# Edge codes of the one-hot comparisons in f32, and the running sums of the last ten attribute batches on VectorE

## What is computed

```python
in_deg = jnp.minimum(jax.ops.segment_sum(ones, dst, num_segments=num_nodes), MAX_IN_DEGREE - 1)
out_deg = jnp.minimum(jax.ops.segment_sum(ones, src, num_segments=num_nodes), MAX_OUT_DEGREE - 1)
edge_proj = edge_attr @ W_sum + b_sum                             # 200000 edges, 128 attributes
sum3d = jax.ops.segment_sum(edge_proj, src, num_segments=num_nodes)
return x + z_in[in_deg] + z_out[out_deg] + cent_term + vor_term + sum3d
```

## Time and profile before

| | us |
|---|---|
| three timed runs | 5856.62, 5861.86, 5867.48 |
| median | 5861.86 |
| profiled execution | 5865.46 |
| its span, first to last instruction | 5863.7 |
| gathers of attribute rows, first to last issue | about 100 to 2163 |
| start of the node stage | about 2213 |

### The profile page before, as it was taken

The page is one execution under the profiler, slowest core; times in us unless marked ns, Lnnn a source line. Parts: engine busy times, 40 slices in busy tenths (PEclk is TensorE's granted clock), DMA queues, the critical chain, the costliest instruction groups (busy, mean ns, idle before and its releaser), DMA issues. The chain is left out here.

```text
span 5863.7 us, 46168 instructions
## 1 busy us (share of the span) xinstructions
PE 3804.6 (65%) x13508; PEld 2479.3 (42%) x13508; DVE 4214.6 (72%) x7748; ACT 1452.0 (25%) x4056; POOL 3577.6 (61%) x3626
## 2 busy tenths in 40 slices
PE   2777777986666655999997344444444444444899
PEld 1655666873444433666665111111111211112666
DVE  8575565559356606877774899999999999996334
ACT  1333333333333332322231111111111111111322
POOL 3777777777777765333321777777777777774000
PEclk9955555555555557999998677777777777776899
DMA  3444444444433332111211888888888888885000
GB/s 86 157 153 145 148 145 153 150 145 151 152 103 104 114 99 61 36 62 62 81 57 67 268 281 282 282 281 283 281 284 280 282 281 282 280 278 181 26 19 25
DMA packets 328215, 968.58 MB, mean 165 GB/s; under 512 B 84412, under 2 KB 124037, under 8 KB 315930
## 3 DMA queue, kind: packets, MB, share of 16 engines
q0 software_dynamic: 198672, 578.35, 32.3%
q1 hardware_dynamic: 80906, 211.35, 10.2%
q10 hardware_dynamic: 48384, 175.92, 7.7%
HBM read 670.63 MB, written 294.73 MB: 165 GB/s over the span
## 5 line engine op out<-in xcount | busy, mean ns | idle before, releaser
L598 POOL DMA_INDIRECT big<-in_edge_attr,big x1568 | 1579.1, 1007 | 573.3 <-issue 474.8
L1777 POOL DMA_INDIRECT big<-keys_values,idx x1674 | 1587.9, 949 | 509.9 <-issue 506.9
L2009 PE MATMUL bank<-big,ident 128*128 128x512 f32 x1674 | 953.1, 735 | 1155.7 <-DVE big L1859 1121.1
L905 PE MATMUL bank<-big,ident 128*128 128x128 f32 x3136 | 1188.0, 482 | 581.2 <-ACT bank L954 522.9
L905 PEld LDWEIGHTS bank<-big,ident 128*128 128x128 f32 x3136 | 777.0, 307 | 914.8 <-ACT bank L954 763.5
L2009 PEld LDWEIGHTS bank<-big,ident 128*128 128x128 f32 x1674 | 389.9, 240 | 1718.3 <-DVE big L1859 1227.3
L954 ACT ACTIVATE bank<-bank,big 128x128 f32<-128x128 f32 x1565 | 535.4, 342 | 1341.6 <-PE bank L905 1329.0
L1881 DVE TENSOR_TENSOR big<-big,bank 128x1536 f32<-128x1536 f32 x279 | 479.8, 1753 | 121.0 <-DMA big<-keys_values,idx 121.0
L651 DVE TENSOR_TENSOR big<-big 128x1024 bf16<-128x1024 bf16 x400 | 276.1, 690 | 342.1 <-PE bank L851 341.6
L1886 DVE TENSOR_REDUCE big<-big 128x48 f32<-128x1536 f32 x279 | 486.8, 1746 | 0.0
L1891 DVE TENSOR_TENSOR big<-big,bank 128x1536 f32<-128x1536 f32 x279 | 478.6, 1744 | 0.0
(11 more groups left out here) (360 smaller groups left out, 4473.2 us busy)
## 6 DMA issues: line engine op xcount, KB each, us to landing
running_sums<-big ACTq DMA_DIRECT2D x196, 512.0 KB, 2.8
running_attention<-big SPq DMA_DIRECT2D x46, 1632.0 KB, 7.6
queries_by_row<-big ACTq DMA_DIRECT2D x139, 512.0 KB
big<-queries_by_row SPq DMA_DIRECT2D x46, 1536.0 KB, 8.8
big<-keys_values,idx POOLq DMA_INDIRECT x1674, 3.9
big<-in_edge_attr,big POOLq DMA_INDIRECT x1568
keys_values<-big SPq DMA_DIRECT2D x7, 1792.0 KB, 7.1
x_after_layer<-big SPq DMA_DIRECT2D x7, 896.0 KB, 4.3
```

The costliest lines, as they stand in the source:

```text
L598: pool.indirect_dma_start(out=z.rows[:, r, k, :], out_offset=None, in_=w["edge_attr_128"][:, :], in_offset=bass.IndirectOffsetOnAxis(ap=z. ...
L905: pe.matmul(sum_of(k), lhsT=m.ident[:, :], rhs=z.rows[:, r, k, :], start=False, stop=True, skip_group_check=True).then_inc(s_sum, 1)
L1777: pool.indirect_dma_start(out=kv[:, r, k, :], out_offset=None, in_=t["kv"][:, :], in_offset=bass.IndirectOffsetOnAxis(ap=m.idx2[:, c:c + 1 ...
L2009: mm = pe.matmul(bank[pair % 4][:, :], lhsT=m.ident[:, :], rhs=kv[:, b % RINGK, i * S + j:(i + 1) * S + j + 1:S, D:KW], start=(j == 0), st ...
```

## The change

`z.nlo` and `z.nhi` are f32 in place of bf16. They take twice the bytes, and the ring of one-hot tables has 8 places in place of 10. The iota table and the one-hot tables remain bf16. Apart from that, the batches 186 to 195 (`DIRECT` = 10) are summed by VectorE: behind its side work one instruction for each column multiplies the sum of the column before by `goes1` and adds the gathered row, from PSUM and SBUF to PSUM. TensorE and ScalarE run their columns up to batch 185; ScalarE then has only the copies and stores of the last ten batches. A copy waits for one column more than it copies. The `due` list is made as before.

```diff
--- before.py
+++ after.py
@@ -54,11 +54,12 @@
 LM = max(PART_COLS)
 B1 = L1 // GB
 RING1 = 4
-RING_OH = 10
+RING_OH = 8
 HI = 50
 COUNTS_PER_TURN = (5, 11)
 READY = -1.0
 RATE = 8.2
+DIRECT = 10
 PLACES = P * L1
 SUMROWS = PLACES + P + 1
 
@@ -351,8 +352,8 @@
     z.zeros, at = cut(m.big, at, 1024)
     z.iota_jt, at = cut(m.big, at, P, GB, dt=BF16)
     z.zb, at = cut(m.big, at, P, dt=BF16)
-    z.nlo, at = cut(m.big, at, EC, dt=BF16)
-    z.nhi, at = cut(m.big, at, EC, dt=BF16)
+    z.nlo, at = cut(m.big, at, EC)
+    z.nhi, at = cut(m.big, at, EC)
 
     z.onehots = []
     for r in range(RING_OH - 2):
@@ -825,6 +826,16 @@
                     due.append(spent)
                 else:
                     spent += cost
+            for b in range(B1 - DIRECT, B1):
+                r = b % RING1
+                dve.wait_ge(s_g[r], 16 * GB * (b // RING1 + 1))
+                for k in range(GB):
+                    c = b * GB + k
+                    dve.wait_ge(s_sum, 2 + c)
+                    if k % GH == 0:
+                        dve.wait_ge(s_copied, 2 * (b - 1) + k // GH + 1)
+                    v.scalar_tensor_tensor(out=sum_of(k), in0=sum_of((k - 1) % GB), scalar=z.goes1[:, c:c + 1],
+                                           in1=z.rows[:, r, k, :], op0=ALU.mult, op1=ALU.add).then_inc(s_sum, 1)
             dve.wait_ge(s_found, 16 * NP1)
             for q in z.tails:
                 tail_places(dve, v, st, q, m.trash1[:, :])
@@ -896,7 +907,7 @@
                     yield
 
             work, placed = shadow(), 0
-            for b in range(B1):
+            for b in range(B1 - DIRECT):
                 r = b % RING1
                 pe.wait_ge(s_g[r], 16 * GB * (b // RING1 + 1))
                 for k in range(GB):
@@ -923,9 +934,9 @@
             qz = t["qrow"][0:ROWS, :].rearrange("(p k) d -> p (k d)", p=P)
             act.wait_ge(s_sum, 2)
 
-            def copy_half(b, k):
+            def copy_half(b, k, further=0):
                 r = b % RING1
-                act.wait_ge(s_sum, 2 + GB * b + GH * (k + 1))
+                act.wait_ge(s_sum, 2 + GB * b + GH * (k + 1) + further)
                 nc.scalar.activation(z.rows[:, r, GH * k:GH * (k + 1), :].rearrange("p k f -> p (k f)"), m.bank[2 + k][:, :],
                                      ACT.Copy).then_inc(s_copied, 1)
 
@@ -958,8 +969,12 @@
                         store(b - 1)
                     if k == GH:
                         copy_half(b, 0)
-            copy_half(B1 - 1, 1)
-            store(B1 - 1)
+            copy_half(B1 - DIRECT - 1, 1, 1)
+            store(B1 - DIRECT - 1)
+            for b in range(B1 - DIRECT, B1):
+                copy_half(b, 0, 1)
+                copy_half(b, 1, int(b < B1 - 1))
+                store(b)
             act.wait_ge(s_zero, 16 * ZEROS)
```

## The result

The changed kernel takes 5939.94 us in the median (5937.27 to 5942.43), the kernel before 5862.1 us in the same comparison: 1.0133 times as long, 95% interval 1.0117 to 1.0149, 78 us slower. The forecast was 5941 us. The profiled execution took 5937.78 us, its span is 5936.0 us against 5863.7.

What follows compares the result with a forecast made beforehand. POOL's unbroken gathers were taken as the bound. Profiled 5865.5 + 100 (held gathers) - 17 (last batches on VectorE) - 4 (ring-slot waits) = 5944.5 us, 3.6 above the median, so 5941 us, range 5880 to 6010.

Steps and rivals of the forecast that it cites:

- The bound: First 2163 us: POOL's gathers, one behind another, set the stage's end; later stages follow in a row.
- The comparisons' length: The 400 counts on VectorE: mixed bf16/f32 comparisons take 1.226 and 0.574 us, from 0.690 and 0.362.
- rival (a): Not slower: mixed comparison keeps 0.690 us or POOL is held no longer than now; 5841 us, chance 0.10.
- VectorE's added work at nothing: In the counts: 299 us more VectorE work fits its idle time and costs nothing, despite the shorter ring.
- The hold: POOL's gathers stand during VectorE instructions with two SBUF operands; longer counts add 69 to 127 us, 100 taken.
- The formula for meetings at random: Each comparison of length T adds (T - 0.17)^2 / 2p to the gathers, p from gather to gather; 46 us before, 173 after.
- Part 2: Last ten batches on VectorE, 0.4 us a column, remove the old chain's lag behind the last gather; 16.9 us gained.
- The ring slots: POOL's 8.7 us of waits for a ring slot: slower gathers take off 0 to 8.7 us, 4 taken.
- The sum: Whole kernel: profiled 5865.5 + 100 - 17 - 4 = 5944.5 us, forecast 5941 us, +1.35%; chance 0.77.
- (b): The two parts nearly cancel, with added hold of 10 to 33 us; 5850 to 5874 us, chance 0.05.
- (c): Counts start as a rule just ahead of a gather, each holding one 1.056 us; 6180 us, chance 0.04.
- (d): VectorE reaches its 80 columns too late and POOL stands; loss up to some 20 us, 5978 us, chance 0.04.

Runs made afterwards that it cites:

- the ring alone: The kernel before with eight tables in the ring in place of ten, codes still bf16; 5854.56 us, ratio 0.9992.
- the table in PSUM: The changed kernel with both comparisons reading the iota table from a PSUM bank; 5826.96 us, ratio 0.9943 to the kernel before.
- the large table in PSUM: bf16 codes, ten tables, last ten batches on VectorE, only the large comparison reading iota from PSUM; 5830.0 us, ratio 0.9948 to the kernel before.
- the upper codes in f32: The kernel before with a ring of eight and only `z.nhi` in f32; 5863.02 us, ratio 1.0006.
- the two runs of part 2 by itself: bf16 codes and ten tables, with the last ten batches (5844.05 us) or the last three (5843.17 us) summed by VectorE.
- part 2 alone: The changed kernel with bf16 codes and ten tables, last ten batches summed by VectorE; 5844.05 us, ratio 0.9971 to the kernel before.

## Why the prediction was right, point by point

**The bound.** POOL's gathers set the stage's end: 100.0 us more busy time there, 94.0 us later at the last gather.

**The comparisons' length.** 1.218 and 0.566 us against 1.226 and 0.574. The mixed pair takes the time of f32, as taken; rival (a) falls. By the formula for f32 tensor_tensor in the Trainium skill, VectorE: DVE Perf Modes, section on the TRN2 errata, the two take an estimated 1.22 and 0.57 us, and the trace agrees.

**VectorE's added work at nothing.** Its wait for tables went from 341.6 to 187.6 us and none of the loss goes by way of TensorE waiting for tables: TensorE is never idle ahead of a count for want of one, the ring alone changed nothing, and with the table in PSUM the equally long comparisons left the kernel faster. The slower gathers were not needed for it: with both tables in PSUM VectorE still waits 108.3 us for tables, and TensorE not once.

**The hold.** 69 to 127 us, 100 taken, 100.0 measured in the gathers' busy time, 102.5 by the rows of the counts alone (162.4 - 59.9). The burst is as worked out (1.62 us a gather, 0.38 of hold); between bursts gathers meet comparisons less regularly. The Trainium skill, SBUF — State Buffer, section "Who interferes with whom", is borne out where it has two SBUF inputs stand against GpSimd's reads, and not in the remark that tensor_tensor stalls no DMA: 159 us of hold went when the second SBUF operand did, and the measurement decides. That the middle was hit to the microsecond is luck: either end was as well supported. The formula for meetings at random gave 46 us before and 173 after, where the rows give 59.9 and 162.4, so that its difference, 127, is too large by some 24 (its 1.48 us from gather to gather stood there without a working; 1.45 is measured and would make it 176). It treats the two comparisons of a count as if they did not touch each other, and they do: in the kernel before the small one held 0.8 us where it gives 5 (in the burst of the earlier trace rows each gather that gets in behind the large one is under way when the small one starts), and in the runs with the large table in PSUM and with the upper codes in f32 the hold moved from one comparison to the other.

**Part 2.** 17 us taken, 16.9 in the trace, 16 and 18 us in the two runs of part 2 by itself. A VectorE column took 0.39 to 0.40 us for the 0.4 taken (0.358 for the instruction alone). What the working left out is that VectorE waits for a whole batch to land, so that its last column ends some 2.8 us later than a column at a time would (seven columns at 0.39 us); POOL's other work covered that.

**The ring slots.** 4 us were taken out of 0 to 8.7; 8.7 went, and 6.0 of POOL's idle time with them, as 0.30 us gaps took their place. But the wait was 3.9 us in the run with the short ring and 0.4 us with part 2 alone, where gathers were not slower. So slower gathers are not what took it away; it looks like scatter from one execution to the next, and should not have stood in the sum.

**The sum.** +94.0 at the last gather and -16.9 behind it make +77.1 at the start of the look-ups; the span grew by 72.3. The missing 4.8 us come off in the later stages, little by little, which the change does not touch; executions of one kernel differ by more (5856.62 to 5867.48), the medians differ by 77.8 us, and no run here looked into it. Rivals (b), (c) and (d) did not come: the hold is 100 us, no gather-by-gather lock at 1.05 us appears in the burst, and VectorE was waiting for its first column 35.66 us ahead of time.

## What to carry to other kernels

Where POOL issues gathers without pause, count VectorE's time in instructions that read all their tensors from SBUF, not its busy time: here a comparison with both operands there held each gather that started well inside it until 0.13 us before its end, and the same work with one operand in PSUM held none. To make one such instruction shorter may only let its neighbour hold more. A change of type that nearly doubles an instruction's length can cost nothing on its own engine and 100 us on another. What comes behind the last transfer is worth taking off, and it is worth the lag and no more: 24 columns did what 80 did.

## What the runs showed of the hardware

A VectorE comparison of one bf16 and one f32 operand runs at the f32 rate (1218 ns for 1024 elements against 690 with both in bf16). With the first operand in PSUM, as f32 and each number repeated eight times by a step of zero, it takes the same time (1212 ns). A gather of 128 rows takes POOL 0.94 us, 1.25 us from start to start, and up to 1.96 us beside a comparison of 1.22 us with both operands in SBUF; a CAST or a TENSOR_SCALAR on one SBUF tensor held gathers as well (11 of 11, 130 of 133). I had not expected the hold to move to the small comparison when the large one stopped holding (the run with only the large table in PSUM lost 29 us of hold where 58 were expected), nor that the chain of running sums stood so close behind POOL: 69 us of waits came up as soon as 159 us of hold were gone.
